# Column maxima of an attention kernel: TensorE transposes replaced by DMA transposes, scores computed ten rows ahead instead of eight

## The chip, the cores and the metric

The kernel runs on one core of a Trainium2 chip. The metric is device time in microseconds (us) of one execution. The kernel before takes 1338.61 us (median of 3 runs, 1338.42 to 1339.37).

## The reference

`x` is (2, 2048, 256) in fp32. Two branches start from the same layer norm `xn` and are added to `x`:

```
z    = layernorm(xn) * g + b
qkv  = z @ w_in.T + b_in           # q, k, v;  then k = q
s    = q k^T / 4                   # 16 heads of width 16, 2 batches: 32 heads of 2048 x 2048 scores
out  = softmax(s) @ v
y    = x + out @ w_out.T + b_out + ffn(xn)     # ffn: 256 -> 1024 -> gelu -> 256, ternary weights
```

Because k = q, each score matrix is symmetric. The softmax needs the maximum of every row of 2048 scores before the exponentials are taken.

## The kernel before

**Stages.** Up to about 233 us of the profiled execution the kernel does layer norm, the q and v projections, the feed-forward branch and the maxima of head 0. From then to about 1270 us it walks the heads; the last head (31) runs in an order of its own, with the output projection between its blocks, until the end.

**One head.** A head's 2048 x 2048 scores are 16 blocks of 128 rows (`kb` = 0 to 15). For block `kb` TensorE writes scores into `pb`, two banks at a time (`b_pair`, x = 0 and 1, line 426). ScalarE turns each pair into exponentials (`prob`, the tile `w`, line 1151: 32 ACTIVATEs a head). TensorE multiplies them by v (`pv_step`, line 414, one block behind). ScalarE also copies out the finished head once (line 1133, after kb = 0 of the next head), and the row of maxima once (`copy_max`, line 1138).

**The maxima of a later head.** Beside head h, the row maxima of head h+1 and the first rows of head h+2 are worked out. `row_step` (line 378) computes for row block i the scores of half of the columns only (8 blocks of 128, or 9 for the i in `WIDE`) into `pr`, one buffer of three banks. VectorE reads them (`row_pass`, line 899): one instruction scales them to fp16 into `planes` and takes the row maximum. The other half of each row is, by symmetry, found as maxima of columns: `columns_step` (line 908) runs an elementwise maximum down the diagonals of `planes`, `columns_round` (line 920) closes the circle. What is left is 16 blocks of 128 x 128 whose maximum is wanted across partitions. `turn_columns` (line 402) transposes them on TensorE, 8 blocks at kb = 8 and 8 at kb = 10, into bank 2, and `fold` (line 926) reduces each 8 blocks on VectorE, after row 1 and row 3 of the following head. Line 932 joins both halves into `neg_max`. GpSimd splits it in two fp16 parts (lines 685, 687), TensorE transposes these at kb = 13, ScalarE copies them after the second exponential of kb = 13, and SyncE's queue writes them beside q (`max_rows_in`, line 575), where the next head's `b_pair` reads them.

**How far ahead.** `ahead_step` issues row step number 16 h + kb + AHEAD at block kb of head h. With AHEAD = 8 the rows 8 to 15 of head h+1 stand at kb = 0 to 7, and the rows 0 to 7 of head h+2 at kb = 8 to 15. Row 0 of a head also waits for that head's q and keys (`s_ld`, "head_loaded").

**Queues.** All engines run in program order and wait on semaphores. There is no scheduler. SyncE's queue carries, for each head h: `load_head(h+2)` (eight DMAs, lines 567 to 570, released when head h-1's score pairs are all issued), `store_o(h-1)` (line 579), in a few heads pieces of the later projection (`sums_in`, `recip_out`, `load_pair`, lines 597 to 611; `load_pair` in heads 20 to 23, 28 and 29), and last `max_rows_in(h+1)`, which waits for `copy_max`. `load_head` reads from `q_dram` with a leading dimension of 2 in four of its eight DMAs (lines 567 and 569, 128 KB each) and 16 partitions in the other four (64 KB each).

## Time and profile before

| | |
|---|---|
| median of 3 runs | 1338.61 us |
| the profiled execution, its own time | 1339.37 us |
| its span in the trace | 1337.5 us |
| PE busy | 1238.3 us (93%) |
| DVE busy | 1181.4 us (88%) |
| ACT busy | 1113.3 us (83%) |
| granted TensorE clock, mean | 0.985 |
| chain that ended last | PE 51%, DVE 20%, ACT 15%, issue 12%, DMA 1% |

PE is TensorE, PEld its weight load, DVE VectorE, ACT ScalarE, POOL GpSimd, SP SyncE (SPq its DMA queue). Busy matmul time is modelled and overlaps from one matmul to the next, so 93% is not TensorE at its peak. Three engines stand between 83% and 93%: what a change is worth has to be read from which of them waits for which.

### The profile page before, as it was taken

Reading aid. Unit: us, or ns where it says so; the run is one execution under the profiler, and the core shown is the slowest. Engines: PE = TensorE matmul, PEld = TensorE weight load, DVE = VectorE, ACT = ScalarE, POOL = GpSimd, SP = SyncE. Lnnn points to the kernel's source line nnn. Section 1 sums busy time; section 2 is a strip of 40 time slices with the busy share of each in tenths; the row PEclk is TensorE's granted clock in tenths of the full one; section 3 lists DMA queues with packets and bytes.
Section 4 is the critical chain, followed back from the end, with each engine's and each line's share of the span. In section 5 each row is a group of like instructions: output and inputs, shape, how many; then the busy total and the mean of one; then the engine's idle time right before and its main releaser. Section 6 shows DMA issues by size and latency. Waiting matters only on the chain.

```text
span 1337.5 us, 25153 instructions
## 1 busy us (share of the span) xinstructions
PE 1238.3 (93%) x9632; PEld 415.8 (31%) x9632; DVE 1181.4 (88%) x1994; ACT 1113.3 (83%) x1260; POOL 137.6 (10%) x215
## 2 busy tenths in 40 slices
PE   7899998699999999999999999999999999999988
PEld 5565653122222222222222222222222222222234
DVE  7777788999999999999999999999999999999543
ACT  5646433599999999999999999999999999999954
POOL 2000000700000000000000000000222200002200
PEclk8999999699999999999999999999999999999999
DMA  6002000000001011110011011112122110121031
GB/s 248 17 17 87 32 17 16 1 33 33 33 33 33 33 33 33 33 33 33 33 33 33 33 33 37 33 37 64 64 65 65 33 35 33 35 65 64 9 129 64
DMA packets 28506, 60.24 MB, mean 45 GB/s; under 512 B 6200, under 2 KB 11736, under 8 KB 28130
## 3 DMA queue, kind: packets, MB, share of 16 engines
q1 hardware_dynamic: 27810, 56.99, 12.5%
q8 instruction: 76, 1.25, 0.4%
q10 hardware_dynamic: 576, 1.65, 0.3%
q14 instruction: 44, 0.36, 0.1%
HBM read 41.29 MB, written 16.77 MB: 43 GB/s over the span
## 4 chain that ended last, share of the span: by engine, by line
PE 51%; DVE 20%; ACT 15%; issue 12%; DMA 1%; DVEq 0%; POOL 0%; ACTq 0%
PE ps L414 19%; ACT w L1151 12%; PE ps L426 12%; DVE score_arena L899 7%; PE ps L378 6%; PE ps L1171 4%; DVE score_arena L908 3%; DVE col_max L926 3%; PE ps L1240 3%; PE ps L1186 2%; PE ps L500 2%; DVE part_max L881 2%; ACT o_evacuated L1133 1%; PE ps L402 1%; DVE score_arena L920 1%
## 5 line engine op out<-in xcount | busy, mean ns | idle before, releaser
L1151 ACT ACTIVATE w<-ps 128x1024 f32<-128x1024 f32 x1024 | 976.2, 1028 | 100.5 <-PE ps L426 72.0
L899 DVE TENSOR_SCALAR_CACHE_REDUCE score_arena<-ps 128x1024 f16<-128x1024 f32 (+1 forms) x496 | 640.0, 1290 | 49.5 <-PE ps L378 40.1
L414 PE MATMUL ps<-w,v_ones 128*32 128x512 f32 x3968 | 530.0, 605 | 5.7 <-ACT o_evacuated L1133 5.7
L426 PE MATMUL ps<-qry,key 50*128 50x512 f16 x1984 | 390.5, 385 | 8.0 <-ACT w L1151 1.4
L908 DVE TENSOR_TENSOR score_arena<-score_arena 128x768 f16<-128x768 f16 (+1 forms) x465 | 276.1, 594 | 0.1
L378 PE MATMUL ps<-qry,key 48*128 48x512 f16 x1426 | 207.0, 327 | 46.5 <-DVE score_arena L899 43.4
L426 PEld LDWEIGHTS ps<-qry,key 50*128 50x128 f16 x1984 | 97.9, 93 | 441.6 <-ACT w L1151 376.3
L414 PEld LDWEIGHTS ps<-w,v_ones 128*32 128x32 f32 x3968 | 79.4, 108 | 138.6 <-issue 137.7
L378 PEld LDWEIGHTS ps<-qry,key 48*128 48x128 f16 x1426 | 68.0, 94 | 131.5 <-DVE score_arena L899 100.8
L677 POOL COPY v_ones<-v_all 128x128 f32<-128x128 f32 x64 | 40.4, 632 | 665.2 <-PE ps L414 665.2
L926 DVE TENSOR_REDUCE col_max<-ps 128x8 f32<-128x1024 f16 x62 | 75.5, 1218 | 3.4 <-PE ps L402 3.4
L1171 PE MATMUL ps<-score_arena,w 128*128 128x256 f16 x512 | 61.7, 278 | 6.2 <-DVE w L875 6.2
L1113 ACT ACTIVATE score_arena<-ps,sigma_bq 128x512 f16<-128x512 f32 x16 | 11.0, 688 | 66.2 <-PE ps L1186 66.2
L875 DVE SCALAR_TENSOR_TENSOR w<-hidden,hidden_scale,w 128x1024 f16<-128x1024 f32 x32 | 40.9, 1283 | 25.5 <-ACT w L1122 25.5
L1240 PE MATMUL ps<-x,score_arena 128*128 128x512 f16 x256 | 61.0, 380 | 0.0
L1171 PEld LDWEIGHTS ps<-score_arena,w 128*128 128x128 f16 x512 | 49.3, 100 | 17.3 <-DVE w L875 7.6
L1117 ACT ACTIVATE hidden<-ps,columns 128x512 f32<-128x512 f32 x64 | 42.3, 681 | 9.2 <-PE ps L1240 7.9
L1019 DVE SCALAR_TENSOR_TENSOR resid<-ps,y_unscale,resid 128x512 f32<-128x512 f32 x16 | 11.9, 746 | 41.2 <-PE ps L500 41.2
L402 PEld LDWEIGHTS ps<-ident_f,score_arena 128*128 128x128 f16 x496 | 27.9, 98 | 52.2 <-issue 52.2
L899 DVE DVE_READ_ACCUMULATOR score_arena<-ps 128x1 f32 x496 | 41.3, 83 | 0.0
L402 PE MATMUL ps<-ident_f,score_arena 128*128 128x128 f16 x496 | 38.4, 220 | 0.2
L1122 ACT ACTIVATE w<-hidden,hidden_scale 128x1024 f16<-128x1024 f32 x32 | 36.7, 1148 | 1.1
(150 smaller groups left out, 634.4 us busy)
## 6 DMA issues: line engine op xcount, KB each, us to landing
key<-q_parts SPq DMA_DIRECT2D x64, 128.0 KB
qry<-q_parts SPq DMA_DIRECT2D x64, 128.0 KB
o_heads<-o_evacuated SPq DMA_DIRECT2D x31, 256.0 KB, 10.2
resid<-in_x SPq DMA_DIRECT2D x8, 512.0 KB, 13.7
q_parts<-score_arena SPq DMA_DIRECT2D x16, 256.0 KB, 2.5
key<-q_parts SPq DMA_DIRECT2D x64, 64.0 KB
qry<-q_parts SPq DMA_DIRECT2D x64, 64.0 KB
out<-resid SPq DMA_DIRECT2D x7, 512.0 KB, 2.6
```

The source lines that it names most:

```text
L378: mm = eng.matmul(pr[:, o:o + size], key[v][r:r + ROWS, i * P:(i + 1) * P], qry[v][r:r + ROWS, c:c + size], start=True, stop=True)
L402: mm = eng.transpose(turned[:, n * P:(n + 1) * P], planes[:, 1, slot(a, (j - 1) % NBLK), :], idh[:, :])
L414: mm = eng.matmul(pv[32 * c:32 * c + 2 * D, :], vst[:, kb, :], prob[kb % 2][:, c * BANK:(c + 1) * BANK], start=(kb == 0), stop=(kb == NBLK ...
L426: mm = eng.matmul(pb[x][:, j * BANK:(j + 1) * BANK], key[v][r:r + KROWS, kb * P:(kb + 1) * P], qry[v][r:r + KROWS, c * BANK:(c + 1) * BANK ...
L875: dve.scalar_tensor_tensor(out=hp[1][:, 2 * i:2 * i + 2, :], in0=hid[:, 2 * i:2 * i + 2, :], scalar=hs[:, 0:1], in1=hp[0][:, 2 * i:2 * i + ...
L899: dve.tensor_scalar(planes[:, 0:w, slot(a, i), :], pr[:, 0:w * P].rearrange("p (b n) -> p b n", n=P), 1.0 / SHIFT, None, ALU.mult, ALU.max ...
L908: dve.tensor_tensor(own, own, planes[:, 2:b + 1, slot(a, i - 1), :], ALU.max).then_inc(s_cw, 1)
L926: dve.tensor_reduce(col_max[:, j0:j0 + SPAN], turned.rearrange("p (j n) -> p j n", n=P), AX.X, ALU.max, negate=True).then_inc(s_ft, 1)
L1117: act.activation(hid[:, f, :], pf[f % 2], ACT.Gelu, scale=1.0 / XS, bias=b1_col[:, f:f + 1]).then_inc(s_g, 1)
L1151: act.activation(prob[kb % 2][:, x * W:(x + 1) * W], pb[x], ACT.Exp, scale=exp_scale).then_inc(s_e, 1)
L1171: mm = pe.matmul(pf[t // 2][:, (t % 2) * C:(t % 2 + 1) * C], hp[i][:, f, t * P:(t + 1) * P], w2t[:, f, :], start=(f == 0 and i == 0), stop ...
L1240: mm = pe.matmul(pf[f % 2], w1t[:, k, f * P:(f + 1) * P], part[:, k, :], start=(k == 0 and i == 0), stop=(k == KC - 1 and i == 1))
```

## The change

The 16 transposes a head leave TensorE. SyncE's queue issues three DMA transposes a head instead (4, 4 and 8 blocks of 128 x 128 fp16), from `planes` into a new tile `columns_t`. VectorE brings the 128 columns of each block to 16 by three elementwise maxima and reduces the rest in one instruction, all after row 5 of the following head, where it also waits for the three DMAs. `planes` has 16 slots instead of 20, so a row pass that reuses a slot waits for the transpose that read it (rows 0, 3 and 7). AHEAD goes from 8 to 10, the rows with nine blocks are others, `copy_max` stands one exponential earlier, and `max_rows_in` is issued ahead of the pieces of the projection.

```diff
-AHEAD = 8
+AHEAD = 10
 MAX_AT = 13
-TURN_AT = (8, 10)
-FOLD_AT = (1, 3)
-WIDE = (8, 9, 10, 11, 12, 13, 14, 15)
+FOLD_AT = 5
+WIDE = (0, 1, 2, 3, 4, 5, 6, 15)
...
-        planes = arena[:, :].rearrange("p (b s n) -> p b s n", b=SPAN + 1, s=SLOTS)
+        planes = arena[:, :].rearrange("p (b s n) -> p b s n", b=SPAN + 1, s=NBLK)
...
+        col_t = sb("columns_t", [P, NBLK, P], F16)
...
-        s_ct = sem("columns_transposed")
+        s_ct = [sem(f"columns_transposed{n}") for n in range(3)]
...
         def slot(a, i):
-            return (NBLK * (a - 1) + i) % SLOTS
+            return (i + 1 + SPAN * (a % 2)) % NBLK
...
-            if i == WIDE[0]:
+            if i == WIDE[-1]:
                 eng.wait_ge(s_mc, a)
...
-        turned = bank(2).bitcast(F16)
-
-        def turn_columns(eng, a, part):
-
-            if part == 0:
-                eng.wait_ge(s_r, NA + NBLK * a)
-                eng.wait_ge(s_cw, NBLK * a - 2)
-            else:
-                eng.wait_ge(s_cw, NBLK * a)
-                eng.wait_ge(s_ft, 2 * a - 1)
-            for n in range(SPAN):
-                j = (SPAN, 0)[part] + n
-                mm = eng.transpose(turned[:, n * P:(n + 1) * P], planes[:, 1, slot(a, (j - 1) % NBLK), :], idh[:, :])
-            mm.then_inc(s_ct, 1)
...
-                if kb in TURN_AT:
-                    turn_columns(eng, h + 1, TURN_AT.index(kb))
...
+            def columns_over(a, n):
+
+                j0, j1 = ((SPAN, SPAN + NCH), (SPAN + NCH, NBLK), (0, SPAN))[n]
+                s0 = (j0 + SPAN * (a % 2)) % NBLK
+                sp.wait_ge(s_cw, NBLK * (a - 1) + (SPAN + NCH - 2, NBLK - 2, NBLK)[n])
+                if n == 0:
+                    wait(sp, s_ft, 4 * (a - 1))
+                sp.dma_start_transpose(col_t[:, j0:j1, :], planes[:, 1, s0:s0 + j1 - j0, :].rearrange("p s n -> p (s n)")).then_inc(s_ct[n], 16)
...
             max_rows_in(0, 0)
+            for n in range(3):
+                columns_over(1, n)
             max_rows_in(1, 1)
...
                     load_head(h + 2, (h + 2) % ROT)
+                if h + 1 < NH:
+                    columns_over(h + 1, 0)
                 store_o(h - 1)
+                if h + 1 < NH:
+                    columns_over(h + 1, 1)
+                    columns_over(h + 1, 2)
+                    max_rows_in(h + 1, (h + 1) % ROT)
                 if h in PIECE_AT:
                     sums_in(PIECE_AT[h])
                 if h - 2 in PIECE_AT:
                     recip_out(PIECE_AT[h - 2])
                 if h in PAIR_AT:
                     load_pair(PAIR_AT[h])
-                if h + 1 < NH:
-                    max_rows_in(h + 1, (h + 1) % ROT)
...
-                if a > 1 and i == SLOTS - NBLK:
-                    dve.wait_ge(s_ct, 2 * (a - 1))
+                if a > 1 and i in (0, NCH - 1, SPAN - 1):
+                    dve.wait_ge(s_ct[(0, NCH - 1, SPAN - 1).index(i)], 16 * (a - 1))
...
-            def fold(a, part):
-                dve.wait_ge(s_ct, 2 * (a - 1) + part + 1)
-                j0 = (SPAN, 0)[part]
-                dve.tensor_reduce(col_max[:, j0:j0 + SPAN], turned.rearrange("p (j n) -> p j n", n=P), AX.X, ALU.max,
-                                  negate=True).then_inc(s_ft, 1)
-                if part:
-                    dve.wait_ge(s_ft, 2 * a)
...
+            def halve(a, n, size):
+                wait(dve, s_ft, 4 * (a - 1) + n)
+                dve.tensor_tensor(col_t[:, :, 0:size], col_t[:, :, 0:size], col_t[:, :, size:2 * size], ALU.max).then_inc(s_ft, 1)
+
+            def fold(a):
+                halve(a, 1, P // 4)
+                halve(a, 2, P // 8)
+                dve.wait_ge(s_ft, 4 * (a - 1) + 3)
+                dve.tensor_reduce(col_max[:, :], col_t[:, :, 0:P // 8], AX.X, ALU.max, negate=True).then_inc(s_ft, 1)
+                dve.wait_ge(s_ft, 4 * a)
...
+                if i == FOLD_AT and a > 1:
+                    for n in range(3):
+                        dve.wait_ge(s_ct[n], 16 * (a - 1))
+                    halve(a - 1, 0, P // 2)
                 if i > 1:
                     columns_step(a, i - 1)
-                if i in FOLD_AT and a > 1:
-                    fold(a - 1, FOLD_AT.index(i))
+                if i == FOLD_AT and a > 1:
+                    fold(a - 1)
...
-                        if x and kb == MAX_AT and not last:
+                        if x == 0 and kb == MAX_AT and not last:
                             copy_max(h + 1)
```

Three places where the instructions stand otherwise. TensorE, in the middle of a head, around row 0 of the head after next (the row that waits for "head_loaded"); line 426 is a score pair, 378 a row step, 414 the product with v, 402 the transposes. Before:

```order
L426 MATMUL ps<-qry,key 128x512 [waits exp_done]
L426 MATMUL ps<-qry,key 128x512
L378 MATMUL ps<-qry,key 128x512 [waits row_max,head_loaded1]
L378 MATMUL ps<-qry,key 128x512
L426 MATMUL ps<-qry,key 128x512 [waits exp_done]
L426 MATMUL ps<-qry,key 128x512
L414 MATMUL ps<-w,v_ones 32x512 [waits exp_done]
L414 MATMUL ps<-w,v_ones 32x512 x3
L402 MATMUL ps<-ident_f,score_arena 128x128 [waits column_max_step,row_max]
L402 MATMUL ps<-ident_f,score_arena 128x128 x7
```

And now (line 411 is the score pair, 399 the product with v):

```order
L378 MATMUL ps<-qry,key 128x512 [waits max_copied,row_max]
L378 MATMUL ps<-qry,key 128x128
L378 MATMUL ps<-qry,key 128x384
L378 MATMUL ps<-qry,key 128x128
L411 MATMUL ps<-qry,key 128x512 [waits exp_done]
L411 MATMUL ps<-qry,key 128x512
L399 MATMUL ps<-w,v_ones 32x512 [waits exp_done]
L399 MATMUL ps<-w,v_ones 32x512 x3
L411 MATMUL ps<-qry,key 128x512 [waits exp_done]
L411 MATMUL ps<-qry,key 128x512
L378 MATMUL ps<-qry,key 128x512 [waits row_max,head_loaded1]
L378 MATMUL ps<-qry,key 128x512
```

The row step that waits for the load stood at kb = 8 and stands at kb = 6; the transposes behind it are gone.

VectorE, rows 0 to 3 of a head before (899 row pass, 908 and 920 column steps, 926 fold, 932 `neg_max`):

```order
L899 TENSOR_SCALAR score_arena,row_max<-ps 128x8x128 [waits column_max_step,pass_a]
L920 TENSOR_TENSOR score_arena<-score_arena 128x896 [waits column_max_step]
L926 TENSOR_REDUCE col_max<-ps 128x8 [waits columns_transposed]
L899 TENSOR_SCALAR score_arena,row_max<-ps 128x8x128 [waits column_max_step,pass_a]
L908 TENSOR_TENSOR score_arena<-score_arena 128x6x128 [waits row_max]
L899 TENSOR_SCALAR score_arena,row_max<-ps 128x8x128 [waits column_max_step,pass_a]
L908 TENSOR_TENSOR score_arena<-score_arena 128x6x128 [waits column_max_step,row_max]
L926 TENSOR_REDUCE col_max<-ps 128x8 [waits columns_transposed]
L932 SCALAR_TENSOR_TENSOR neg_max<-row_max,col_max 128x16 [waits max_split_pool,row_max,columns_folded]
```

VectorE, row 5 of a head now, up to row 6 (897 row pass, 918 the halvings, 906 column step, 924 the reduction, 928 `neg_max`):

```order
L897 TENSOR_SCALAR score_arena,row_max<-ps 128x9x128 [waits column_max_step,pass_a]
L918 TENSOR_TENSOR columns_t<-columns_t 128x16x64 [waits columns_transposed2,columns_folded,columns_transposed1,columns_transposed0]
L906 TENSOR_TENSOR score_arena<-score_arena 128x7x128 [waits column_max_step,row_max]
L918 TENSOR_TENSOR columns_t<-columns_t 128x16x32 [waits columns_folded]
L918 TENSOR_TENSOR columns_t<-columns_t 128x16x16 [waits columns_folded]
L924 TENSOR_REDUCE col_max<-columns_t 128x16 [waits columns_folded]
L928 SCALAR_TENSOR_TENSOR neg_max<-row_max,col_max 128x16 [waits max_split_pool,row_max,columns_folded]
L897 TENSOR_SCALAR score_arena,row_max<-ps 128x9x128 [waits column_max_step,pass_a]
```

The two folds stood two rows apart among rows of eight blocks; their successor is one run of five instructions between two rows of nine blocks.

SyncE's queue in a head with `load_pair`, now (550 to 553 the head load, 567 the transposes, 571 `store_o`, 558 `max_rows_in`, 604 and 605 `load_pair`); before, the four DMAs of `load_pair` stood between `store_o` and `max_rows_in`:

```order
L567 DMA_TRANSPOSE columns_t<-score_arena 128x4x128 [waits columns_folded,column_max_step]
L571 DMA o_heads<-o_evacuated 128x512 [waits o_evacuated]
L567 DMA_TRANSPOSE columns_t<-score_arena 128x4x128 [waits column_max_step]
L567 DMA_TRANSPOSE columns_t<-score_arena 128x8x128 [waits column_max_step]
L558 DMA qry<-max_rows 2x16x128 [waits max_copied]
L558 DMA qry<-max_rows 2x16x128
L604 DMA below_half<-o_heads 128x1x512 [waits recip_stored]
L605 DMA weight_scratch<-o_recip 128x1x512
L604 DMA below_half<-o_heads 128x1x512
L605 DMA weight_scratch<-o_recip 128x1x512
L550 DMA key<-q_parts 32x1x2048 [waits pass_b]
```

`load_pair` moved from behind the head load of its own head to right ahead of the next one.

## Rows read from the trace of the kernel before

**Rows 1.** Line 1133, once a head: nanoseconds min/median/max, first and last start.

```profile
L1133 ACT ACTIVATE o_evacuated<-ps x31: 597/603/603, 285.6 to 1270.4; 128x512 f32<-128x512 f32 x31
```

**Rows 2.** Groups by shape, 285.6 to 1270.4 us: busy us, mean ns, idle before.

```profile
L1151 ACT ACTIVATE w<-ps 128x1024 f32<-128x1024 f32 x961 | 913.9, 1028 | 56.6 <-PE ps L426 54.0
L899 DVE TENSOR_SCALAR_CACHE_REDUCE score_arena<-ps 128x1152 f16<-128x1152 f32 x239 | 324.4, 1357 | 24.7 <-PE ps L378 21.5
L908 DVE TENSOR_TENSOR score_arena<-score_arena 128x896 f16<-128x896 f16 x210 | 132.1, 629 | 0.1
L926 DVE TENSOR_REDUCE col_max<-ps 128x8 f32<-128x1024 f16 x60 | 73.1, 1218 | 3.4 <-PE ps L402 3.4
L920 DVE TENSOR_TENSOR score_arena<-score_arena 128x512 f16<-128x512 f16 x6 | 2.5, 422 | 0.0
L932 DVE SCALAR_TENSOR_TENSOR neg_max<-row_max,col_max 128x16 f32<-128x16 f32 x30 | 5.2, 174 | 1.0
```

**Rows 3.** Line 885, a short reduction (32 elements a partition).

```profile
L885 DVE TENSOR_REDUCE neg_max<-part_max x1: 187/187/187, 231.9 to 231.9; 128x16 f32<-128x32 f32 x1
```

**Rows 4.** Timeline of one head, 708 to 728 us: start, us, engine, line.

```profile
708.73 0.62 SPq L567 DMA_DIRECT2D key<-q_parts  x1
...
712.35 15.14 ACT L1151 ACTIVATE w<-ps 128x1024 f32<-128x1024 f32 x16
...
713.26 0.42 SPq L579 DMA_DIRECT2D o_heads<-o_evacuated  x1
...
720.20 1.36 DVE L899 TENSOR_SCALAR_CACHE_REDUCE score_arena<-ps 128x1152 f16<-128x1152 f32 x1
...
721.62 0.45 PE L378 MATMUL ps<-qry,key 48*128 48x512 f16 x4
722.10 1.36 DVE L899 TENSOR_SCALAR_CACHE_REDUCE score_arena<-ps 128x1152 f16<-128x1152 f32 x1
...
725.12 0.39 PE L426 MATMUL ps<-qry,key 50*128 50x512 f16 x2
...
727.06 0.62 PE L402 MATMUL ps<-ident_f,score_arena 128*128 128x128 f16 x8
```

**Rows 5.** Stretches of that head: second last number is the DMA engines' share.

```profile
722.25:722.50 0.25, 0.25 (x5) 0.12 (x8) 0.25 (x1) 0.25 (x1) 0.00 (x0) 1.00 0.13 49
722.50:722.75 0.25, 0.25 (x8) 0.00 (x0) 0.25 (x1) 0.25 (x2) 0.00 (x0) 1.00 0.07 25
```

**Rows 6.** `o_heads`: DMA from issue to landing, min/median/max.

```profile
DMA to landing us min/median/max: 2.0/10.2/11.4
```

**Rows 7.** The first three head loads: first and last issue on SyncE's queue.

```profile
104.01 0.65 SPq L567 DMA_DIRECT2D key<-q_parts  x1
...
126.71 1.99 SPq L570 DMA_DIRECT2D qry<-q_parts  x1
```

**Rows 8.** The DMA engines' share behind them.

```profile
134.00:142.00 8.00, 8.00 (x63) 7.45 (x62) 5.29 (x17) 2.17 (x4) 0.00 (x0) 0.84 0.13 53
142.00:143.00 1.00, 1.00 (x12) 0.89 (x10) 0.68 (x3) 0.00 (x0) 0.83 (x1) 1.00 0.07 26
```

**Rows 9.** Timeline, rows ahead of head 0's first score pair.

```profile
233.16 0.39 PE L378 MATMUL ps<-qry,key 48*128 48x512 f16 x2
...
246.98 0.64 PE L426 MATMUL ps<-qry,key 50*128 50x512 f16 x2
```

**Rows 10.** SyncE's queue in head 20, the first with `load_pair`.

```profile
906.33 0.62 SPq L567 DMA_DIRECT2D key<-q_parts  x1
...
914.06 2.70 SPq L611 DMA_DIRECT2D weight_scratch<-o_recip  x1
936.54 1.40 SPq L575 DMA_DIRECT2D qry<-max_rows  x2
939.11 0.61 SPq L567 DMA_DIRECT2D key<-q_parts  x1
```

**Rows 11.** Head 20, the end of the DMA engines' work.

```profile
926.00:927.00 1.00, 1.00 (x12) 0.16 (x10) 1.00 (x1) 1.00 (x2) 0.00 (x0) 1.00 0.09 35
```

More of the change, by code:

```diff
@@ L65, in attention_ffn @@
     SPAN = NBLK // 2
-    SLOTS = NBLK + 4
     SCALE = 1.0 / float(D) ** 0.5
@@ L84, in sem @@
             return ctx.enter_context(nc.semaphore(name))
-        arena = sb("score_arena", [P, (SPAN + 1) * SLOTS * P], F16)
-        planes = arena[:, :].rearrange("p (b s n) -> p b s n", b=SPAN + 1, s=SLOTS)
+        PLANE = NBLK * P
+        arena = sb("score_arena", [P, (SPAN + 1) * PLANE], F16)
+        planes = arena[:, :].rearrange("p (b s n) -> p b s n", b=SPAN + 1, s=NBLK)
         def part_of(kb, size, dt=F32):
@@ L914, in columns_round @@
                 j0 = slot(a, 0)
[L915 to L933 removed]
+                own = planes[:, 1, j0:j0 + b - 1, :]
+                dve.tensor_tensor(own, own, planes[:, 2:b + 1, slot(a, i), :], ALU.max).then_inc(s_cw, 1)
+            def halve(a, n, size):
[7 more added lines that the diff above has]
+                dve.wait_ge(s_ft, 4 * a)
+                dve.wait_ge(s_r, NA + NBLK * a)
+                dve.wait_ge(s_mp, 2 * a)
+                dve.scalar_tensor_tensor(out=neg_max[:, :], in0=row_max[:, a % 2, :], scalar=-1.0, in1=col_max[:, :],
+                                         op0=ALU.mult, op1=ALU.min).then_inc(s_m, 1)
             def between(a, i):
@@ L1010, in _ @@
             columns_round(NH - 1)
-            for part in range(len(FOLD_AT)):
-                fold(NH - 1, part)
+            for n in range(3):
+                dve.wait_ge(s_ct[n], 16 * (NH - 1))
+            halve(NH - 1, 0, P // 2)
+            fold(NH - 1)
             def add_y(n, lasts):
```

11 lines of the change are left out of this document (removed).

## The prediction, made before the changed kernel ran

> **What bounds the kernel now.** I read the busy shares and the chain of the page first. Three engines are above 80% busy, and the chain passes from one to the other, so no single engine sets the time; what counts is how long one head takes and which waits fill it. Line 1133 runs once a head: 31 times from 285.6 to 1270.4, so a head takes 984.8 / 30 = 32.83 us [rows 1]. Then the groups by shape. ScalarE's 16 exponentials in a row took 15.14 us, 0.946 each [rows 4], so 32 need 30.3, and with the copy-out of 0.60 [rows 1] ScalarE needs 30.9 of the 32.83. The reader should see that its idle time, 56.6 us over 30 heads, ends nearly always with TensorE's scores [rows 2]. TensorE in turn waits for VectorE, because the row scores have one buffer: in a stretch of nine-block rows one row pass begins at 720.20 and the next at 722.10, 1.90 a block [rows 4], against 2 x 0.946 = 1.89 for ScalarE. The three engines are level within 1%; the 1.9 us a head above ScalarE's need come where VectorE has a fold beside the rows and TensorE its transposes. Last I read the DMA side: the engines' share in one head, and how long the stores take to land. That view decides my forecast.
>
> **The change, part by part.** Sums are made against the profiled execution, 1339.4 us (a span of 1337.5 and 1.9 around it); it is 0.8 above the median of 1338.6.
>
> *Folds and transposes.* Two folds of 1218 ns go, 2.44 us a head [rows 2]. In their place come elementwise maxima over 1024, 512 and 256 elements a partition and a reduction of 256. The rows have 422 ns for 512 elements and 629 for 896, so 0.54 ns an element: 0.70, 0.42 and 0.28 [rows 2]. The reduction, between 187 ns for 32 elements [rows 3] and 1218 for 1024 [rows 2], is 1.04 ns an element: 0.42. Together 1.82, so VectorE has 0.62 less a head. TensorE loses two runs of transposes of 0.62 busy each [rows 4], 1.2 a head at most. Against that, the two folds stood apart among eight-block rows, where VectorE has some room; now 1.82 and the 0.17 of `neg_max` [rows 2] stand nearly in one piece (one column step, due anyway, is between them) among nine-block rows of 1.90, where it has none. What such a piece can cost: eight nine-block rows at 1.90, eight other blocks at ScalarE's 1.89, the piece of 2.0, the copy-out 0.6 give 32.9, the head as it is. The other end is ScalarE's need, 30.9, or 1.9 less. The same addition for the kernel before (2.44 + 0.17 instead of 2.0) gives 33.5, which is 0.7 more than it takes, so the addition overstates and only its difference, 0.6, should be believed. I take 0.4 less a head, since one long piece is absorbed worse than two short ones: 30 heads, -12 us (from -57 to +12, taking 0.4 the wrong way as the bad end).
>
> *Ten rows ahead and the head load.* Row 0 of head h+2 waits for `load_head(h+2)`, which is issued as head h begins. Before, that row stands at kb = 8; its block begins at 725.12 [rows 4], 16.4 us after the first DMA of the load at 708.73. Now it stands at kb = 6. The row step of kb = 6 ran at 721.62, so 12.9 after the issue. When does the load land? The DMA engines show a share of 0.13, that is two engines of sixteen, until about 722.6 [rows 5]. The store of 256 KB issued behind the load at 713.26 [rows 4] lands 10.2 us later in the median, where one with nothing ahead lands in 2.0 [rows 6]: 723.5. The tail is the load's: the first three loads, with no store among them, are issued from 104.01, and the share stands at 0.13 up to 142 and falls in the slice after it [rows 7, 8], some 38 us for three, 12.7 each. Of the 722.6 the store's own part on the two engines is some 0.6 (16 KB each at half of the 49 GB/s of rows 5), so the load's bytes end at 722.0, and with the 0.8 between last byte and landing (723.5 less 722.7) it lands at 722.8, 14.1 after its issue. TensorE comes 1.2 us too early, and with TensorE in order the score pair and the product behind the row step wait too. ScalarE has one exponential in hand, and I let 0.3 of the wait be hidden: +0.9 a head, 29 heads, +26 us. The ends are 0 (the load is ready by kb = 6) and 1.4 a head, +41.
>
> The Trainium skill states, in "DMA: Bandwidth & Descriptors", Rules for kernel authors, that the number of engines of a DMA follows its slowest dimension and that an outermost dimension under 16 confines it to that many. The load's leading dimension is 2, and the two busy engines agree.
>
> *The DMA transposes.* The trace has none, so their landing is bounded by neighbours. The first one is issued behind the head load, at about 713.5 as the store is now, and stands in the same queues: it can't land before the load. If it spreads like the store its 128 KB are 8 KB an engine, 0.3 us more, 723.1. Row 0's scores are ready for VectorE 0.45 (the row step, rows 4) after TensorE's late start at 722.8, at 723.25: no further wait. If it is confined like the load, to two engines at 24.5 GB/s each, it takes 2.6 us, and VectorE waits 2.2 more a head, +63 in all. The second and third have four rows each before their use, 7.6 us, and the DMA engines are empty by then. The store is the nearer row (128 partitions in both), so I take 0.
>
> The Trainium skill gives 1309 ns for one 128x128 block by the DMA crossbar ("VectorE: DVE Perf Modes", The three transpose paths), and in "Advanced Engine Details and Errata", X-Bar Transpose (TRN2), says that transposes are as fast as regular DMAs. By the first, 4 blocks would be an estimated 5.2 us and 8 blocks 10.5; no row of this trace can decide between them.
>
> *Before head 0.* Eight rows run from 233.16 until the first score pair at 246.98 [rows 9], 1.73 each and more towards the end. Two more, and seven of the ten with nine blocks (a nine-block row pass is 1.36 against 1.23 in an eight-block one): 2 x 2.0 + 7 x 0.13 = +5 us. It isn't given back, since the last heads run at ScalarE's pace without rows; the missing transposes of head 30 give about -1.
>
> *The moved pieces of the projection.* In the heads with `load_pair` the DMA engines are busy until about 926.4 [rows 11], 20.1 after the load's issue at 906.33 [rows 10]; without it it was 13.9. So the four DMAs put 6.2 us on the two engines. Now they are issued after `max_rows_in`, which ended at 936.54 + 1.40 = 937.94 [rows 10] and comes one exponential earlier, at 937.0. The next head load, due at 939.11, finds the two engines busy until 937.6 + 6.2 = 943.8; its first packets would have started at about 940.3. It lands 3.5 late, and the row at kb = 6 is already waiting: 3.5 us in each of five heads (21 to 24 and 29), less what those heads hid: +15 (from 0 to +25). `copy_max` and `max_rows_in` a microsecond earlier I cost at nothing: exponentials run on either side.
>
> Sum: 1339.4 - 12 + 26 + 0 + 5 - 1 + 15 = 1372. Against the median of the runs that is 33 us or 2.5% slower.
>
> **The rivals.** *The load is no obstacle, and the folds pay* (faster). Its place is the wait for the load at kb = 6. It decides at a landing 12.9 us after the issue: if the load's own part of the two-engine tail is shorter than I make it, or the first blocks of a head get slower so that kb = 6 comes later, nothing waits. Then 1339.4 - 12 + 5 - 1, with little from the pairs: 1331; with the full 1.2 a head off TensorE, 36 instead of 12, 1307. I put it at 1328. For it speaks that the margin is 1.2 us in 14; against it, that two separate stretches of the trace give the same 12 to 13 us for a load.
>
> *The transposes are slow* (slower by far). If one holds the queue far longer than a store of its size, VectorE waits at row 0 every head, and the third may be late for row 5. With the two-engine price it is 1372 + 63 = 1435. For it: no row shows one at all. Against it: 512 KB a head is less than the load and the store move now.
>
> By the 1309 ns a block of the Trainium skill's page ("VectorE: DVE Perf Modes", The three transpose paths) the queue would need an estimated 21 us a head for them, the third DMA would miss row 5, and the time would pass 1500; I count this within this rival, with a third of its chance.
>
> *Gains and waits cancel*: a load wait of 0.4 a head (12 us) against the fold's 12, and nothing in the pairs: 1339.
>
> **How the numbers follow.** Load wait as forecast 0.48, slow transposes 0.20, no obstacle 0.24, cancelling 0.08. The forecast's own range, from the ends of the load wait, the pairs and half the fold's range, is 1345 to 1395. For 8 in 10 I take 1322 to 1445: it leaves out half of the slow case and a part of the fast one. This kernel's runs tell some 0.2% (2.7 us) from no change. Faster 0.24, same 0.08, slower 0.68.
>
> **What would show it.** Right: TensorE idle about 1 us once a head before a row step, ended by the DMA into q or keys; line 1133 every 33.3 us or so, more in heads 21 to 24; VectorE's idle small at row 0; the reduction near 0.4 us. Wrong: the period at or below 32.8, or VectorE's largest wait on `columns_t`, which is the slow case. A period of 32.4 with no DMA wait on TensorE makes the landing time the failed step; a wait of 3.5 us missing in head 21 makes it the pairs.

## The result, and the profile after

The changed kernel takes 1436.84 us (median of 4 runs, 1431.64 to 1439.88) against 1338.99 for the kernel before on the same chip (4 runs): a ratio of 1.0724 [1.0685, 1.0763]. It is 98 us slower, where 33 were forecast. The profiled execution has a span of 1431.2 us and a mean granted clock of 0.956. The page's busy times, clock and chain first (before: 93%, 88%, 83% and a chain of 1% DMA):

```profile
PE 1242.5 (87%) x9136; PEld 395.0 (28%) x9136; DVE 1167.1 (82%) x2050; ACT 1119.0 (78%) x1260; POOL 122.8 (9%) x215
...
PEclk9999997899999999999999999999989899999999
...
PE 33%; DMA 22%; DVE 20%; issue 18%; ACT 4%; SPq 2%; DVEq 1%; POOL 0%; ACTq 0%; POOLq 0%
```

The busy microseconds hardly changed (TensorE +4, VectorE -14, ScalarE +6), and DMA has come into the chain. For VectorE and ScalarE the 94 us of longer span are idle time. TensorE's +4 hides two things: its transposes (38.4 us) are gone, and its other matmuls take longer, the products with v alone 20 us (the first two lines are of before, the third of after):

```profile
L402 PE MATMUL ps<-ident_f,score_arena 128*128 128x128 f16 x496 | 38.4, 220 | 0.2
L414 PE MATMUL ps<-w,v_ones 128*32 128x512 f32 x3968 | 530.0, 605 | 5.7 <-ACT o_evacuated L1133 5.7
...
L399 PE MATMUL ps<-w,v_ones 128*32 128x512 f32 x3968 | 550.0, 626 | 5.6 <-ACT o_evacuated L1135 5.6
```

The copy-out once a head, now line 1135, answers to [rows 1]:

```profile
L1135 ACT ACTIVATE o_evacuated<-ps x31: 597/603/628, 288.4 to 1364.0; 128x512 f32<-128x512 f32 x31
```

A head takes (1364.0 - 288.4) / 30 = 35.85 us, where it took 32.83. So +90.8 us of the 93.7 lie in the heads, +2.8 ahead of them and +0.1 behind. From the copy-out's starts in the timeline, the five heads 21 to 24 and 29 (the "pair heads" below: their load is issued behind `load_pair`) go from 164.8 to 207.8 (+43.0) and the other 25 from 820.0 to 867.8 (+47.8). Groups by shape over 288 to 1364 us answer to [rows 2]:

```profile
L918 DVE TENSOR_TENSOR columns_t<-columns_t 128x1024 f16<-128x1024 f16 x30 | 20.6, 687 | 3.3 <-DMA columns_t<-score_arena 3.3
L918 DVE TENSOR_TENSOR columns_t<-columns_t 128x512 f16<-128x512 f16 x30 | 12.5, 418 | 0.0
L918 DVE TENSOR_TENSOR columns_t<-columns_t 128x256 f16<-128x256 f16 x30 | 8.8, 292 | 1.0
L924 DVE TENSOR_REDUCE col_max<-columns_t 128x16 f32<-128x256 f16 x30 | 12.6, 420 | 1.0
```

The four new VectorE instructions cost 687 + 418 + 292 + 420 = 1.82 us, exactly as forecast. The waits (total us, times, longest):

```profile
ACT w L1153 <- PE ps L411: 113.2, 99, 18.5
...
PE ps L378 <- DVE score_arena L897: 75.5, 47, 1.8
...
PE ps L378 <- DMA qry<-q_parts: 56.8, 29, 7.2
DVE score_arena L897 <- DMA columns_t<-score_arena: 50.3, 25, 7.0
```

Both waits that the forecast and its slow rival had named are there: TensorE for the head load (29 times), and VectorE for the transposes. An ordinary head shows them (timeline: start, us, engine, line; in brackets the idle time before it):

```profile
705.04 0.61 SPq L550 DMA_DIRECT2D key<-q_parts  x1
...
710.31 1.22 SPq L567 DMA_TRANSPOSE columns_t<-score_arena  x1
...
718.62 0.44 PE L378 MATMUL ps<-qry,key 48*128 48x512 f16 x3 [0.58 <-DMA qry<-q_parts]
...
719.24 1.36 DVE L897 TENSOR_SCALAR_CACHE_REDUCE score_arena<-ps 128x1152 f16<-128x1152 f32 x1 [0.88 <-DMA columns_t<-score_arena]
```

The load lets TensorE go on 13.6 us after its issue (forecast 14.1). Of the 56.8 us, 29.9 are waited in the five pair heads and 26.9 in 24 others, 1.12 in each (forecast 1.2). VectorE's wait is booked on the transpose, but the scores it needs were only ready at about 719.1, so some 0.1 of the 0.88 is the transpose's own. In this head the two waits are mostly one and the same time; g1 below tests it for the rest.

The third thing is one I had not forecast. The mean granted clock falls below 0.98 in 15 of the 30 heads, in none before. Two neighbouring heads (us, PE, PEld, DVE, ACT, POOL busy, PEclk, DMA share, GB/s):

```profile
528.70:562.40 33.70, 30.50 (x242) 7.72 (x239) 30.53 (x54) 31.09 (x35) 1.19 (x5) 1.00 0.43 48
562.40:600.70 38.30, 33.38 (x242) 7.75 (x239) 30.59 (x54) 31.18 (x35) 1.23 (x5) 0.91 0.38 44
```

They hold the same instructions; the second is 4.6 us longer. Late in a head with such a drop (head 12), matmuls that else take 0.39, 0.39 and 1.06 run so:

```profile
700.89 0.61 PE L411 MATMUL ps<-qry,key 50*128 50x512 f16 x2
...
701.29 0.63 PE L378 MATMUL ps<-qry,key 48*128 48x512 f16 x2
...
702.28 1.93 PE L399 MATMUL ps<-w,v_ones 128*32 128x512 f32 x8
```

Heads at full clock take 33.7 to 34.3 us (30.8 the last), heads with a drop 34.8 to 38.3, and the five pair heads, all with a drop, 40.4 to 43.0. The clock in these traces shows where it falls. In the heads of this run it falls 20 times: 12 times behind the idle stretch of 1.78 us that TensorE has after the fold's run, 6 times at its wait for the head load (the five pair heads and head 12), and twice behind a late row pass shortly after row 0.

So three suspects, and the experiments take them away one at a time: the head load confined to two DMA engines, the place of the nine-block rows with the fold's run among them, and the moved pieces of the projection. A fourth, the DMA transposes themselves, was the rival whose figure (1435) the measured time hits; g1 shows that it hits it by chance.

### The profile page after: what moved, and what is told of

Read it like the earlier page. It is cut to its first block, busy times and chain, and to the rows that moved or that the text cites. A ratio compares the mean times of both kernels' runs of the same rounds, so it can differ in the third digit from the quotient of the medians.

```text
span 1431.2 us, 24369 instructions
## 1 busy us (share of the span) xinstructions
PE 1242.5 (87%) x9136; PEld 395.0 (28%) x9136; DVE 1167.1 (82%) x2050; ACT 1119.0 (78%) x1260; POOL 122.8 (9%) x215
## 2 busy tenths in 40 slices
DMA packets 94968, 76.46 MB, mean 53 GB/s; under 512 B 72664, under 2 KB 78200, under 8 KB 94594
## 3 DMA queue, kind: packets, MB, share of 16 engines
q1 hardware_dynamic: 94274, 73.26, 35.9%
## 4 chain that ended last, share of the span: by engine, by line
PE 33%; DMA 22%; DVE 20%; issue 18%; ACT 4%; SPq 2%; DVEq 1%; POOL 0%; ACTq 0%; POOLq 0%
DMA columns_t<-score_arena 15%; PE ps L399 10%; PE ps L411 6%; DMA qry<-q_parts 6%; DVE score_arena L906 6%; DVE score_arena L897 5%; PE ps L378 4%; PE ps L1173 3%; DVE columns_t L918 3%; PE ps L1242 3%; ACT w L1153 2%; PE ps L1188 2%; DVE part_max L879 2%; PE ps L483 2%; PE ps L464 1%
## 5 line engine op out<-in xcount | busy, mean ns | idle before, releaser
L897 DVE TENSOR_SCALAR_CACHE_REDUCE score_arena<-ps 128x1152 f16<-128x1152 f32 (+1 forms) x496 | 640.1, 1290 | 154.8 <-PE ps L378 92.0
L399 PE MATMUL ps<-w,v_ones 128*32 128x512 f32 x3968 | 550.0, 626 | 5.6 <-ACT o_evacuated L1135 5.6
L411 PE MATMUL ps<-qry,key 50*128 50x512 f16 x1984 | 407.0, 397 | 7.1 <-ACT w L1153 1.1
L378 PE MATMUL ps<-qry,key 48*128 48x512 f16 x1426 | 214.0, 338 | 134.8 <-DVE score_arena L897 75.5
L906 DVE TENSOR_TENSOR score_arena<-score_arena 128x768 f16<-128x768 f16 (+1 forms) x465 | 281.6, 606 | 0.1
L411 PEld LDWEIGHTS ps<-qry,key 50*128 50x128 f16 x1984 | 112.1, 94 | 527.5 <-ACT w L1153 433.9
L675 POOL COPY v_ones<-v_all 128x128 f32<-128x128 f32 x64 | 25.6, 401 | 756.6 <-PE ps L399 756.6
L1140 ACT ACTIVATE max_rows<-ps 32x128 f16<-32x128 f16 x32 | 8.5, 267 | 65.1 <-PE ps L388 65.1
L918 DVE TENSOR_TENSOR columns_t<-columns_t 128x1024 f16<-128x1024 f16 (+2 forms) x93 | 43.3, 466 | 4.3 <-DMA columns_t<-score_arena 3.3
L879 DVE TENSOR_REDUCE part_max<-ps 128x1 f32<-128x1024 f32 x32 | 37.5, 1214 | 0.0
## 6 DMA issues: line engine op xcount, KB each, us to landing
resid<-in_x SPq DMA_DIRECT2D x8, 512.0 KB, 14.1
```

Of the source, the lines that this page charges most:

```text
L378: mm = eng.matmul(pr[:, o:o + size], key[v][r:r + ROWS, i * P:(i + 1) * P], qry[v][r:r + ROWS, c:c + size], start=True, stop=True)
L399: mm = eng.matmul(pv[32 * c:32 * c + 2 * D, :], vst[:, kb, :], prob[kb % 2][:, c * BANK:(c + 1) * BANK], start=(kb == 0), stop=(kb == NBLK ...
L411: mm = eng.matmul(pb[x][:, j * BANK:(j + 1) * BANK], key[v][r:r + KROWS, kb * P:(kb + 1) * P], qry[v][r:r + KROWS, c * BANK:(c + 1) * BANK ...
L879: dve.tensor_reduce(part_max[:, a // 2, a % 2:a % 2 + 1], pa[a % 2], AX.X, ALU.max).then_inc(s_r, 1)
L897: dve.tensor_scalar(planes[:, 0:w, slot(a, i), :], pr[:, 0:w * P].rearrange("p (b n) -> p b n", n=P), 1.0 / SHIFT, None, ALU.mult, ALU.max ...
L906: dve.tensor_tensor(own, own, planes[:, 2:b + 1, slot(a, i - 1), :], ALU.max).then_inc(s_cw, 1)
```

## The experiments

The four columns on the right are of each run's profiled execution; a head "with a drop" is one whose mean granted clock is below 0.98. Before's medians beside these runs lie between 1339.0 and 1339.9. The head load starts out as four DMAs with a leading dimension of 2 and four of 16 partitions.

| run | median us | ratio to before [interval] | us a head | pair heads (5) | other heads (25) | heads with a drop |
|---|---|---|---|---|---|---|
| before | 1339.4 | | 32.83 | 164.8 | 820.0 | 0 |
| after | 1436.8 | 1.0724 [1.0685, 1.0763] | 35.85 | 207.8 | 867.8 | 15 |
| e1_spread | 1376.5 | 1.0300 [1.0266, 1.0335] | 33.70 | 169.6 | 841.3 | 19 |
| e2_pieces | 1421.8 | 1.0624 [1.0601, 1.0647] | 35.37 | 183.9 | 877.3 | 17 |
| e3_ahead8 | 1344.3 | 1.0036 [1.0020, 1.0053] | 33.07 | 175.4 | 816.7 | 5 |
| e4_wide | 1395.4 | 1.0431 [1.0399, 1.0464] | 34.61 | 204.8 | 833.4 | 6 |
| g1_copy | 1426.5 | 1.0631 [1.0604, 1.0658] | 35.65 | 207.8 | 861.6 | 15 |
| g2_copy_undone | 1320.3 | 0.9859 [0.9843, 0.9876] | 32.19 | 160.7 | 805.1 | 2 |
| g3_copy_wide | 1318.8 | 0.9845 [0.9829, 0.9861] | 32.04 | 160.6 | 800.4 | 0 |
| h1_copy_nine | 1372.5 | 1.0231 [1.0195, 1.0268] | 33.90 | 170.6 | 846.5 | 26 |
| f2_before_ahead10 | 1384.5 | 1.0339 [1.0322, 1.0356] | 34.14 | 176.0 | 848.2 | 4 |
| f3_before_ahead10_spread | 1342.3 | 1.0023 [1.0012, 1.0033] | 32.79 | 165.2 | 818.6 | 0 |
| g4_before_late | 1357.2 | 1.0118 [1.0096, 1.0140] | 33.54 | 185.7 | 820.5 | 4 |
| e8_before_late_spread | 1342.0 | 1.0022 [1.0013, 1.0032] | 32.93 | 167.4 | 820.6 | 0 |

**e1_spread.** After, with the load in twelve DMAs of 16 partitions each:

```diff
-sp.dma_start(key[v][r:r + 2 * D, :], src).then_inc(s_ld[v], 16)
+for p in range(2):
+    sp.dma_start(key[v][r + p * D:r + (p + 1) * D, :], src[p]).then_inc(s_ld[v], 16)
```

(The same for `qry`, and 192 in place of 128 in the waits.)

> The changed kernel, with the head load's four DMAs of leading dimension 2 cut into eight of 16 partitions each (12 DMAs a head instead of 8), so that the load is no longer confined to two DMA engines. Theory, the load's two-engine tail: TensorE's wait for the load (56.8 us in 29 heads) and most of VectorE's wait for the first DMA transpose (50.3 us in 25 heads, queued behind the load) go; quiet heads fall from 33.9 to about 32.4 us and the heads after load_pair from 41.5 to about 37: some 1375 us. Rival, the DMA transposes themselves are slow: VectorE's wait on columns_t stays near 2 us a head, only TensorE's wait goes, and the time stays above 1410.

Measured 1376.5: 60 us less. TensorE's wait for the load falls from 56.8 us in 29 to 4.8 in 5, and VectorE's wait at the row pass for `columns_t` is gone, though the transposes are the same. In the heads it is 38 us from the pair heads and 27 from the others. What stays is 37 us above before, with 19 heads of some 34.0 us at a clock of 0.95, beside five of 32.6; in all 19 the clock falls behind the 1.78 us of idle TensorE after the fold's run. The confined load, with what it does to the pair heads, is the greatest single part, and VectorE's wait was its consequence.

**e2_pieces.** After, with the three pieces of the projection back behind `store_o`:

```diff
 store_o(h - 1)
+if h in PIECE_AT: sums_in(PIECE_AT[h])
+if h - 2 in PIECE_AT: recip_out(PIECE_AT[h - 2])
+if h in PAIR_AT: load_pair(PAIR_AT[h])
 ...
 max_rows_in(h + 1, (h + 1) % ROT)
-if h in PIECE_AT: sums_in(PIECE_AT[h])          # and the other two
```

> The changed kernel with the pieces of the projection (load_pair, sums_in, recip_out) put back behind store_o, ahead of the second DMA transpose; max_rows_in is last again. Theory, load_pair ahead of the head load delays it: heads 21 to 24 and 29, which took 40.4 to 43.0 us, fall to about 35, some 38 us less: about 1398. Rival, those heads are long for another reason (GpSimd's normalisation, the queue's depth): they keep over 39 us, and the time stays above 1425.

Measured 1421.8, 15 us less, not 39. The five pair heads gave back 24 of their 43; the others were 9.5 longer in this profile, with 17 drops instead of 15.

**e3_ahead8.** After, as far ahead and with the nine-block rows as before:

```diff
-AHEAD = 10
-FOLD_AT = 5
-WIDE = (0, 1, 2, 3, 4, 5, 6, 15)
+AHEAD = 8
+FOLD_AT = 3
+WIDE = (8, 9, 10, 11, 12, 13, 14, 15)
```

(The row that waits for `copy_max` moves with the table, here to row 8; in e4, g2 and g3 it moves likewise, and TensorE is in no list of waits for that copy.)

> The changed kernel at AHEAD = 8, with the nine-block rows 8 to 15 as before and the fold after row 3 (the same place in TensorE's order), DMA transposes kept. Theory, the two rows more ahead expose the load: TensorE's wait for the load disappears in quiet heads, the first transpose has 3.8 us more and VectorE waits for it no longer, the third has only two rows before its use and costs up to 1 us a head; the heads after load_pair lose 4 us: 1370 to 1385. Rival, the transposes are what costs: VectorE waits on columns_t for 3 us or more a head at the fold and the time is 1430 or more.

Measured 1344.3, 93 us less and better than either side expected. Most heads now take 32.12, 0.7 under before's usual 32.78, with all the DMA transposes in place. The load is late in the five pair heads alone (8.0 us). The transposes aren't free here, though: three of the five drops (heads 9, 16 and 27, together 11 us longer than 32.12) stand where the fold, after row 3, waits for the transposes (the load ahead of them is still confined), here in head 9:

```profile
563.40 0.69 DVE L918 TENSOR_TENSOR columns_t<-columns_t 128x1024 f16<-128x1024 f16 x1 [1.42 <-DMA columns_t<-score_arena]
```

That one table of numbers holds two of the causes (load wait and place of the nine-block rows), so this run alone doesn't part them; the next ones do.

**e4_wide.** After, ten rows ahead, with most nine-block rows moved away from the fold's run:

```diff
-WIDE = (0, 1, 2, 3, 4, 5, 6, 15)
+WIDE = (0, 1, 10, 11, 12, 13, 14, 15)
```

> The changed kernel with the nine-block rows moved to 10 to 15, 0 and 1, so that the run of five instructions after row 5 stands among eight-block rows, as the folds did before. Theory, this run among nine-block rows idles TensorE long enough for its clock to fall to half in a good part of the heads (mean granted clock 0.956, heads of 35.4 to 38.3 us against 33.8): those heads fall to 33.8 or less, 20 to 35 us less in all, mean clock above 0.97. Rival, the clock falls because of the waits at row 0: no change within 0.5%, the clock as it is.

Measured 41 us less, drops in 6 heads instead of 15 and the mean clock at 0.968. TensorE still waits 57.2 us for the load in 29 heads. None of its falls of the clock stands behind the fold's run any more; five are in the pair heads, at the wait for the load. So the two causes are separate, and the second has to do with the clock.

**f2_before_ahead10 and f3_before_ahead10_spread.** The kernel before, TensorE transposes and all, ten rows ahead; f3 spreads the load as well.

```diff
-AHEAD = 8
-MAX_AT = 13
-TURN_AT = (8, 10)
+AHEAD = 10
+MAX_AT = 12
+TURN_AT = (6, 8)
```

> The kernel before with AHEAD = 10 alone (TensorE transposes, at kb = 6 and 8 and the maxima at kb = 12, so that they follow the same rows as before). Theory, the two rows more ahead expose the head load without any DMA transpose: TensorE waits 1 to 1.3 us for the load at row 0 of 29 heads, heads of about 33.9 us, 1339.4 + 30 + 4 ahead of head 0 = 1370 to 1375. Rival, the load only lands late because the transposes delay it or because the changed heads are shifted: no wait for the load, 1338 to 1346.

> The same (the kernel before, AHEAD = 10 alone) with the head load cut into 12 DMAs of 16 partitions. Theory, the load's two-engine tail is the cause: the wait goes, 1340 to 1346. Rival, ten rows ahead cost for another reason (the wait of the first nine-block row for copy_max, the two rows before head 0): as slow as without the cut.

f2 measured 1384.5, 45 us above before, and f3 1342.3. The wait that was forecast stands by itself in f2's waits:

```profile
PE ps L378 <- DMA qry<-q_parts: 37.0, 29, 2.2
```

That is 1.28 us a head; 1.2 was forecast. The 25 ordinary heads became 28 us longer, two of them (20 and 28) with a drop. The 22 that wait and have no drop wait 24.0 us and became 21.7 longer, so of the 0.3 a head that I had let ScalarE hide, 0.1 was real. The five pair heads became 11 longer.

**g1_copy.** After, with each DMA transpose replaced by a plain DMA copy of the same blocks. The column maxima are then those of untransposed blocks, and the scores are scaled 256 times smaller; g2, g3 and h1 share this.

```diff
-sp.dma_start_transpose(col_t[:, j0:j1, :], planes[:, 1, s0:s0 + j1 - j0, :].rearrange("p s n -> p (s n)"))
+sp.dma_start(col_t[:, j0:j1, :], planes[:, 1, s0:s0 + j1 - j0, :])
```

> The changed kernel with each DMA transpose replaced by a plain DMA copy of the same bytes between the same tiles (the column maxima are then taken of untransposed blocks, so the maxima are not those of the columns; the exponent's scale is 256 times smaller, which keeps the numbers finite and the instructions the same). Theory, what a transpose waits for is the queue behind the head load, and its own cost is small: VectorE's wait at row 0 (50.3 us) shrinks to little more than half, TensorE's wait for the load stays at 1 to 2 us a head, the time is 1400 to 1430. Rival, the crossbar transposes are the main cost: the waits on columns_t vanish, the later waits for the load too, and the time is below 1380.

Measured 1426.5, only 10 us less, with 15 drops as before. Its waits for the load:

```profile
PE ps L378 <- DMA qry<-q_parts: 58.1, 29, 6.4
```

VectorE's 50.3 us on `columns_t` are gone from the list, and the time has hardly moved: it now stands under "waits for TensorE's scores" (136.9 instead of 92.0). The plain copies too land late, when they stand behind the confined load (the first line is g1's; the second is of g3 below, with the same copies and the load spread):

```profile
DMA to landing us min/median/max: 2.0/2.3/14.6
...
DMA to landing us min/median/max: 2.0/2.2/4.0
```

So the transposing costs some 10 of the 98 us; with the intervals of both ratios it is 6 to 19. The slow-transposes rival falls, though its figure was right to 2 us.

**g2_copy_undone and g3_copy_wide.** With the copies, both delays undone in two ways: g2 by the spread load, the pieces back and `AHEAD` = 8 with the table of e3; g3 by the spread load, the pieces back and the table of e4, still ten rows ahead.

> The same plain copies with AHEAD = 8 (nine-block rows 8 to 15, fold after row 3), the head load on all engines, and the pieces of the projection behind store_o. Theory, moving the turning of the columns off TensorE and folding in SBUF is worth 0.66 us a head once nothing delays the heads: all heads near 32.12, some 1318 to 1322. Rival, some heads (9, 16, 27 took 36 us in the AHEAD = 8 run with transposes) stay long for a reason outside the transposes and the load: 1330 or more.

> The same plain copies, load on all engines and pieces behind store_o, but with AHEAD = 10 and the fold after row 5 as in the changed kernel, and the nine-block rows at 10 to 15, 0 and 1. Theory, the clock drops of the spread-load run (19 heads at 34.0 us against 32.6) come from the fold's run standing among nine-block rows: no head below a mean clock of 0.98, heads of 32.1 to 32.6 us, 1322 to 1335. Rival, the drops come with ten rows ahead or with transposes in any place: 1350 or more, or (if the transposes are what drops it) no way to tell from this run alone.

Measured 1320.3 and 1318.8, 1.4 and 1.6% under before; both intervals stay clear of 1, though the gain is less than 2%. g2 has two drops left (heads 9 and 27, behind its fold as in e3, though with plain copies), g3 none. This is what the new path is worth with its obstacles gone and the crossbar's own cost left out. With the 6 to 19 us of g1 added, an estimate for a version that transposes is 1325 to 1338, at or a little under before. No run shows that version.

**h1_copy_nine.** g3 with the nine-block rows back where the change had put them, and with them the row that waits for `copy_max` (15 instead of 10).

```diff
-WIDE = (0, 1, 10, 11, 12, 13, 14, 15)
+WIDE = (0, 1, 2, 3, 4, 5, 6, 15)
```

> The run of plain copies with AHEAD = 10, load on all engines and pieces behind store_o (1318.8 us), with one thing put back as the changed kernel has it: the nine-block rows are 0 to 6 and 15 (and the numbers again wrong in the same way, with the exponent's scale 256 times smaller). Nothing waits for a DMA and no transpose is in it. Theory, the fold's run after row 5 among nine-block rows idles TensorE and drops its clock: most heads at 34.0 us with a mean clock of 0.95, some 1360 to 1375. Rival, it was the transposes or the load behind it that dropped the clock: heads of 32.0 to 32.6, 1318 to 1340.

Measured 1372.5: 54 us from that table, on a kernel in which nothing waits for the head load and `columns_t` is waited for once, for 2.5 us. The number of nine-block rows is the same, and TensorE never waits for `copy_max` in either. h1 differs from e1 only by plain copies for transposes and the pieces put back, and is 4 us below it: with the load spread, those two together cost little. Here is the end of the fold's run in g3 (920 the halvings, 926 the reduction, 899 the row pass, 411 a score pair, 1142 `copy_max`):

```profile
628.43 0.42 DVE L926 TENSOR_REDUCE col_max<-columns_t 128x16 f32<-128x256 f16 x1
...
628.99 1.23 DVE L899 TENSOR_SCALAR_CACHE_REDUCE score_arena<-ps 128x1024 f16<-128x1024 f32 x1
...
630.28 0.39 PE L378 MATMUL ps<-qry,key 48*128 48x512 f16 x2 [1.36 <-DVE score_arena L899]
...
631.08 0.27 ACT L1142 ACTIVATE max_rows<-ps 32x128 f16<-32x128 f16 x1 [1.10 <-PE ps L388]
```

And in h1:

```profile
653.50 0.42 DVE L926 TENSOR_REDUCE col_max<-columns_t 128x16 f32<-128x256 f16 x1
...
654.06 1.36 DVE L899 TENSOR_SCALAR_CACHE_REDUCE score_arena<-ps 128x1152 f16<-128x1152 f32 x1
...
655.48 0.61 PE L378 MATMUL ps<-qry,key 48*128 48x512 f16 x2 [1.78 <-DVE score_arena L899]
...
656.46 1.98 PE L399 MATMUL ps<-w,v_ones 128*32 128x512 f32 x8
656.77 0.27 ACT L1142 ACTIVATE max_rows<-ps 32x128 f16<-32x128 f16 x1 [2.00 <-PE ps L388]
...
658.38 0.57 PE L411 MATMUL ps<-qry,key 50*128 50x512 f16 x2
```

TensorE idles 0.4 us longer behind the run, and in h1 its matmuls after it take 0.61 for 0.39 and 1.98 for 1.06. The stretches with their clock, g3 and then h1 (columns as above; PEclk is the third from the end):

```profile
627.87:629.87 2.00, 1.05 (x10) 0.10 (x2) 1.90 (x5) 2.00 (x3) 0.41 (x2) 1.00 0.00 0
629.87:631.87 2.00, 1.59 (x15) 0.33 (x15) 1.98 (x6) 0.90 (x3) 0.00 (x0) 1.00 0.00 0
631.87:633.87 2.00, 2.00 (x22) 0.60 (x19) 1.93 (x6) 1.99 (x3) 0.00 (x0) 1.00 0.04 8
```

```profile
652.42:654.42 2.00, 1.29 (x10) 0.15 (x10) 1.90 (x6) 2.00 (x3) 0.20 (x1) 1.00 0.00 0
654.42:656.42 2.00, 0.94 (x4) 0.13 (x4) 1.83 (x4) 0.35 (x1) 0.22 (x1) 0.74 0.00 0
656.42:658.42 2.00, 2.00 (x13) 0.31 (x13) 1.48 (x3) 1.17 (x2) 0.00 (x0) 0.50 0.00 0
658.42:660.42 2.00, 2.00 (x17) 0.44 (x16) 1.21 (x3) 1.43 (x2) 0.00 (x0) 0.91 0.04 8
```

In g3 TensorE is busy 2.64 us of 4 around the run, and the clock stays at full. In h1 it is busy 2.23 of 4, and by the clock column it runs some 3.4 us at 0.50, the lower level of 1.2 GHz (1.0 of the stretch at 0.74, all of the next, 0.4 of the last). ScalarE, which needs TensorE's scores, is busy only 2.6 of the 4 us from 656.42. That head took 34.13 us, g3's 31.97. h1's one ordinary head at full clock took 32.63, so of the 2.1 us of such a head the drop is 1.4 to 1.5 and the nine-block rows around the run, without a drop, 0.7. In all 26 heads with a drop the clock falls behind this idle stretch of 1.78 us.

**g4_before_late and e8_before_late_spread.** The kernel before with nothing changed but the three pieces put behind `max_rows_in`; e8 spreads the load as well.

```diff
-if h in PIECE_AT: sums_in(PIECE_AT[h])          # and the other two
 max_rows_in(h + 1, (h + 1) % ROT)
+if h in PIECE_AT: sums_in(PIECE_AT[h])          # and the other two
```

> The kernel before with one part of the change: the pieces of the projection are issued after max_rows_in, right ahead of the next head load. Theory, the load of heads 21 to 24 and 29 lands 3.5 to 6 us later, 17.5 to 20 us after its usual issue time, past row 0 at kb = 8 (16.4 us): those heads take 1 to 4 us more, 1344 to 1358 in all. Rival, at AHEAD = 8 the load has room enough and the cost in the changed kernel was that of ten rows ahead with the transposes: no change (1338 to 1341).

> The kernel before with the pieces of the projection issued after max_rows_in (1357.2 us alone, +17.5) and the head load cut into 12 DMAs of 16 partitions. Theory, load_pair hurts only because it stands in front of a load that is confined to two engines: the load on all engines lands in time in heads 21 to 24 and 29 too, 1338 to 1343. Rival, it is SyncE's issue of the four DMAs or GpSimd's late normalisation that holds these heads: 1350 or more.

g4 measured 1357.2, +18, all in the five heads (164.8 to 185.7), four of them with a drop. TensorE's waits for the load are about half of the 21 us; in the four the clock falls at these waits:

```profile
PE ps L378 <- DMA qry<-q_parts: 11.3, 5, 3.1
```

e8 measured 1342.0: with a spread load the late pieces cost 2 or 3 us. So the moved pieces cost this much only where the load is confined; the extra in after (43) comes with both delays falling on the same wait, 6.0 us a pair head instead of g4's 2.3, and with the clock that falls at it.

## Why the prediction was wrong in size

The sign and the first mechanism held; the sum was 33 and should have been 98. The heads hold 91 us of it. With the load spread (e1) 26 of the 91 stay, where the fold's term had put -12: 38 off. The other 65 go when the load is spread: 38 in the pair heads, where load and pieces together had been put at 19.5 (15, and five times 0.9), and 27 in the others, where 22 had been put (24 times 0.9). So two terms were mis-sized: the fold's, and that of the pieces. Neither counted TensorE's clock. That 1436.8 lies within the wide range of 1322 to 1445 is luck, since the range reached so far only for slow transposes. Point by point:

*Folds replaced, -12: the instructions right, the absorption wrong.* The price of 1.82 us was met to the hundredth. Where the path is free they give even more than 0.4 a head: the usual head takes 32.12 in e3 and 31.97 in g3, 0.7 and 0.8 less than 32.78. What failed is the sentence that one long piece among nine-block rows is "absorbed worse", priced at 0.2 us a head, with 0.4 the wrong way as its bad end. Its place costs 1.9 us a head in the mean and 2.1 in a head with a drop (h1 against g3), and that is the greatest error of the sum. It isn't the length of the piece: g3 has it in one piece too, among eight-block rows, with no drop and 31.97 us a head. I had added up VectorE's time and ScalarE's and had not asked what TensorE does meanwhile. It stands idle behind the run, and the lower clock that follows prolongs everything it feeds.

*The head load, +26: right in the ordinary heads.* Landing 14.1 forecast, 13.6 to 14.6 seen in the 24 that wait; a wait of 1.2 forecast, 1.12 in after and 1.28 in f2. In after the 25 ordinary heads give 27 us back when the load is spread. f2 is 45 us above before, not 26, since little is hidden and four heads have a drop. Spreading the load gives 60 back in after, 42 in f2, 15 in g4.

*The rule on engines.* The trace before had two busy engines, and the runs now bear out what follows: cut into DMAs of 16 partitions, the same 768 KB hold TensorE up for 4.8 us in e1 instead of 56.8. The Trainium skill ("DMA: Bandwidth & Descriptors", Rules for kernel authors) has it as a rule that the slowest dimension sets the number of engines. The cut that follows from it was worth 60 us in e1.

*The DMA transposes, 0: nearly right.* They cost 6 to 19 us by g1, of the 0 to 63 that I had allowed. They go out in 1.2 us and land in 3 (e1, with the load ahead of them spread):

```profile
DMA to landing us min/median/max: 2.4/3.0/8.0
```

In after it is 2.4/3.5/16.0. By size, in e1's median 4 blocks land in 2.4 us and 8 in 3.0; the plain copies of the same bytes in h1 take 2.1 and 2.3. The Trainium skill says that transposes are as fast as regular DMAs ("Advanced Engine Details and Errata", X-Bar Transpose (TRN2)). These landings are near it, if a little above. By the Trainium skill's 1309 ns for one block ("VectorE: DVE Perf Modes", The three transpose paths), 4 or 8 blocks would be an estimated 5.2 or 10.5 us, which these landings don't show.

*The moved pieces, +15: mis-sized.* In after the five pair heads cost 43 more, for pieces and load together; 19.5 was forecast. The next load is issued at 1023.90 and TensorE gets on with it 19.3 us later:

```profile
1020.91 0.63 SPq L604 DMA_DIRECT2D below_half<-o_heads  x1
...
1023.90 0.64 SPq L550 DMA_DIRECT2D key<-q_parts  x1
...
1043.17 0.71 PE L378 MATMUL ps<-qry,key 48*128 48x512 f16 x3 [6.31 <-DMA qry<-q_parts]
```

My own working gave 17.6 (14.1 and 3.5 late); the five loads take 17.5 to 19.5. TensorE waits 6.3 us here, 29.9 in the five heads, and then it runs at half clock until about 1049 (the matmul takes 0.71 for 0.44), which the forecast did not count:

```profile
1040.00:1044.00 4.00, 0.83 (x5) 0.28 (x5) 0.08 (x1) 0.00 (x0) 0.00 (x0) 0.50 0.71 125
1044.00:1048.00 4.00, 4.00 (x21) 0.83 (x23) 2.48 (x4) 2.28 (x3) 0.00 (x0) 0.50 0.03 4
1048.00:1052.00 4.00, 4.00 (x30) 0.77 (x22) 3.22 (x7) 3.04 (x4) 0.77 (x1) 0.88 0.34 66
```

Alone (g4) they cost 18, near the forecast's 15, but that is luck: at eight rows ahead row 0 comes 16.4 us after the issue, so a landing at 17.6 would cost only 1.2 in each of five heads, 6 in all. There the load lands at 17.4 to 18.7, the waits are 11.3 us, and the rest comes with the drops.

*The prologue, +5, and the tail, -1:* +2.8 and +0.1.

*The sign that I had named for the slow case was bad.* I had written that VectorE's largest wait on `columns_t` would show slow transposes. That wait appeared (50.3 us), and g1 took it away for 10. A wait is booked on whatever came last, by however little.

What stays open: how the drops in after are spread over the heads (15 of 30 in one profile, 15 in g1, 19 with the load spread) I can't derive; no run shows what decides between two heads with the same instructions. Taken one at a time out of after the causes give 60, 41, 15 and 10, which is 126. All four taken out together (g3) give 118, so they add up to within 8 us; 98 is less than that because the new path itself gains 20. The split depends on the order all the same: the nine-block rows' place is worth 41 with the load confined (e4) and 54 with it spread (h1 to g3), and no run shows why.

## What to carry to other kernels

When three engines are level, price a serial run on one of them by what the others do meanwhile: TensorE's idle time behind it can cost as much as the run itself (2.1 us in h1's heads against a run of 2.0), by way of the clock. Before work that needs a load is brought forward, spread that load over all DMA engines; here that edit made ten rows ahead nearly free (3 us in f3, 45 in f2). Don't read a wait's booked releaser as its cause until a run has replaced that releaser by something cheaper.
